# Cross-attention and expert layer: one token tile and one value tile per attention step, and one row-maximum instruction for both heads of a step

## The reference, cut to what matters

```python
x = x + tanh(g_xattn[0]) * xattn(layernorm(x), ctx_1024, Wq, Wk, Wv, Wo, bo)   # (8, 512, 512), 8 heads of 64
x = x + tanh(g_ffn[0])   * moe(layernorm(x), gate_w, Wu, Wv, Wo)               # 8 experts, rank 128, 2 chosen per token

# xattn
q, k, v = x @ Wq, context @ Wk, context @ Wv        # split into 8 heads of 64
attn = softmax(q k^T / 8)                           # 512 x 512 per batch row and head
out  = (attn v) @ Wo + bo
```

## Time and profile before

| what | value |
|---|---|
| median of 3 runs | 1095.46 us (1092.81 to 1096.62) |
| the profiled execution, its own time | 1095.08 us |
| its span in the trace | 1093.3 us |
| TensorE busy | 901.7 us, 82% of the span |
| VectorE busy | 682.8 us |
| ScalarE busy | 571.8 us |
| GpSimd busy | 540.2 us |
| attention steps 0 to 31 in the trace | from 51.3 us to about 767 us |

### The profile page before, as it was taken

The page is one execution under the profiler, slowest core; times in us unless marked ns, Lnnn a source line. Parts: engine busy times, 40 slices in busy tenths (PEclk is TensorE's granted clock), DMA queues, the critical chain, the costliest instruction groups (busy, mean ns, idle before and its releaser), DMA issues.

```text
span 1093.3 us, 22768 instructions
## 1 busy us (share of the span) xinstructions
PE 901.7 (82%) x8210; PEld 547.0 (50%) x8210; DVE 682.8 (62%) x1595; ACT 571.8 (52%) x1022; POOL 540.2 (49%) x645
## 2 busy tenths in 40 slices
PE   4888988998998899899899989986640999799890
PEld 2344444555455455455555545544320787677660
DVE  5677776677687767867767776685334454444440
ACT  3367656666457555655754655656120564555450
POOL 6222253353565466447545544547463246556564
PEclk9999999999999999999999999999765899899995
DMA  8455734645453264354336226643343589899986
GB/s 264 143 165 176 236 117 99 191 108 127 128 145 74 66 192 108 67 174 113 74 91 200 69 59 189 185 117 125 103 145 116 139 186 197 167 187 187 196 143 84
DMA packets 125997, 154.52 MB, mean 141 GB/s; under 512 B 48448, under 2 KB 81216, under 8 KB 125120
## 3 DMA queue, kind: packets, MB, share of 16 engines
q1 hardware_dynamic: 109024, 115.67, 37.0%
q0 software_dynamic: 16864, 37.40, 17.8%
HBM read 67.06 MB, written 56.56 MB: 113 GB/s over the span
## 4 chain that ended last, share of the span: by engine, by line
PE 53%; DVE 13%; DMA 10%; issue 9%; ACT 7%; POOL 4%; SPq 2%; POOLq 1%; ACTq 0%; DVEq 0%
PE G L1244 27%; DMA out_dram<-V,Ph 8%; PE ST L1301 4%; PE ST L1300 4%; PE MX L1286 3%; PE MX L1468 3%; PE G L1253 3%; POOL out_dram L673 3%; DVE mx L884 2%; PE PV L1317 2%; PE PV L1313 2%; PE PV L1315 2%; DVE tiles L874 2%; PE G L1460 1%; ACT Ph L708 1%
## 5 line engine op out<-in xcount | busy, mean ns | idle before, releaser
L630 POOL TENSOR_TENSOR Pl<-P,Ph 128x512 f16<-128x512 f32 x128 | 153.4, 1202 | 215.5 <-ACT Ph L708 215.0
L705 ACT ACTIVATE P<-ST 128x512 f32<-128x512 f32 x256 | 153.3, 599 | 201.4 <-PE ST L1301 166.8
L884 DVE TENSOR_REDUCE mx<-MX 128x1 f32<-128x512 f32 x256 | 168.2, 684 | 26.7 <-PE MX L1286 26.7
L708 ACT ACTIVATE Ph<-ST 128x512 f16<-128x512 f32 x256 | 154.3, 603 | 0.4
L673 POOL DMA_INDIRECT out_dram<-V,Ph x78 | 122.1, 1566 | 47.4 <-ACT V L841 30.1
L1468 PE MATMUL MX<-heads,tiles 128*128 128x256 f16 x936 | 121.5, 283 | 18.5 <-DVE heads L1198 18.2
L1313 PE MATMUL PV<-V,Ph 128*128 128x65 f16 x1024 | 114.4, 195 | 12.2 <-issue 12.2
L1317 PE MATMUL PV<-V,Pl 128*128 128x65 f16 x1024 | 114.4, 194 | 2.7 <-issue 2.6
L1315 PE MATMUL PV<-V,Ph 128*128 128x64 f16 x1024 | 114.6, 197 | 0.9 <-issue 0.9
L1313 PEld LDWEIGHTS PV<-V,Ph 128*128 128x128 f16 x1024 | 97.5, 98 | 34.3 <-issue 16.5
L1468 PEld LDWEIGHTS MX<-heads,tiles 128*128 x936 | 92.3, 101 | 41.4 <-issue 23.0
(11 more groups left out here) (206 smaller groups left out, 1895.4 us busy)
## 6 DMA issues: line engine op xcount, KB each, us to landing
heads<-expert_rows SPq DMA_DIRECT2D x39, 516.0 KB
tiles<-in_x_dram SPq DMA_DIRECT2D x32, 256.0 KB, 5.1
tiles<-in_ctx_dram SPq DMA_DIRECT2D x32, 256.0 KB, 5.2
second_norm<-in_x_dram SPq DMA_DIRECT2D x32, 256.0 KB, 3.2
out_dram<-second_norm SPq DMA_DIRECT2D x32, 256.0 KB, 2.3
heads<-q_hi SPq DMA_DIRECT2D x124, 64.0 KB
heads<-k_hi SPq DMA_DIRECT2D x124, 64.0 KB
expert_rows<-zero_rows SPq DMA_DIRECT2D x8, 516.0 KB, 5.3
```

What stands on the lines that cost most here:

```text
L630: nc.gpsimd.tensor_tensor(Pl[:, hh, c, :], P32[:, c, :], Ph[:, hh, c, :], ALU.subtract).then_inc(pl_pool, 1)
L705: nc.scalar.activation(P32[:, c, :], ST[:, c % 2, :], ACT.Exp, scale=0.125 / SC2).then_inc(p_ready, 1)
L708: nc.scalar.activation(Ph[:, hh, c, :], ST[:, c % 2, :], ACT.Exp, scale=0.125 / SC2).then_inc(ph_ready, 1)
L884: nc.vector.tensor_reduce(out=mx[:, k // TT, k % TT:k % TT + 1], in_=MX[:, (k + odd) % 2, :], axis=AXX, op=ALU.max).then_inc(mx_taken, 1)
```

## The change

Four things are done together.

1. **Token and value tiles.** From step 2 on every step prepares one token tile (tile g + 6) and, from step 4 on, one value tile (tile g + 4); steps 0 and 1 keep two token tiles, steps 2 and 3 two value tiles. The sums over the kernel are the same. The token tile's x transposes stand after S6, its context transposes after half of the weighted sums, the value tile at the end of the step. Loads, layernorm statistics and factors are made tile by tile, not batch row by batch row.
2. **Row maxima.** The two heads' products of a token block are issued one behind the other into the two banks, each over its own 64 partitions, and one VectorE instruction reduces both banks (128 x 2 x 512). Four reductions stand where eight stood. The low part of k no longer enters the maximum.
3. **Order around the general banks.** The output projection, the ranks and the tiles change places in `bank_uses`; the transpose of the maxima stands before the logits; in steps j = 1 the ranks follow the output projection. On ScalarE the high part of oT moves behind one more pair of exponentials, and the high parts of the tile behind another.
4. **Ranking on VectorE.** `best_two` moves from before the low part of oT to after the token tile's low parts; `places` moves from the end of step j = 1 into step j = 2, after two of the four reductions.

```diff
+def token_tiles(g, steps):
+
+    first, second = ([4 + 2 * g], [5 + 2 * g]) if g < 2 else ([g + 6], [])
+    return [n for n in first if n < steps], second
+
+
+def value_tiles(g, steps):
+
+    if g < 4:
+        return [2 * g, 2 * g + 1] if g >= 2 else []
+    return [g + 4] if g + 4 < steps else []
...
@@ bank_uses
+        first, second = token_tiles(g, steps)
+        names += [(z, n) for n in first for z in "xc"]
+        if b:
+            names.append(("out", g - 4))
+        names += [(z, n) for n in second for z in "xc"]
         if j == 1 and b >= 2:
             names.append(("ranks", b - 2))
-        if b:
-            names.append(("out", g - 4))
-        names += second
+        names += [("v", n) for n in value_tiles(g, steps)]
...
@@ vector engine
-            def row_max(n, k, odd):
-                dve.wait_ge(mx_filled, n + 1)
-                nc.vector.tensor_reduce(out=mx[:, k // TT, k % TT:k % TT + 1], in_=MX[:, (k + odd) % 2, :], axis=AXX,
+            def row_max(n, t):
+
+                dve.wait_ge(mx_filled, n)
+                nc.vector.tensor_reduce(out=mx[:, :, t:t + 1].rearrange("p h o -> p (h o)"), in_=MX[:], axis=AXX,
                                         op=ALU.max).then_inc(mx_taken, 1)
...
@@ tensor engine
             def row_max_scores(g, k):
...
-                h, t = k // TT, k % TT
+                t, h = divmod(k, 2)
+                rows_ = slice(h * HD, (h + 1) * HD)
                 if k == 0:
                     pe.wait_ge(qk_dma[s], turn * QK_DMAS * 16)
                 if k == 1:
                     since(pe, mrow_ready, g)
                 else:
-                    since(pe, mx_taken, g * (2 * TT) + k - (1 if k > 1 else 0))
-                nc.tensor.matmul(MX[:, (k + g) % 2, :], Q1[:, s, h, t * P:(t + 1) * P], K1[:, s, h, :],
+                    since(pe, mx_taken, g * TT + t)
+                nc.tensor.matmul(MX[:, h, :], Q1[rows_, s, h, t * P:(t + 1) * P], K1[rows_, s, h, :],
                                  start=True, stop=True).then_inc(mx_filled, 1)
...
@@ tensor engine, step
-                    maxima(2 * k)
+                    maxima(2 * k, 2 * k + 1)
...
-                maxima(2 * k + 1)
...
                 scores(b, j, 4)
                 last_head(2, 3)
+                scores(b, j, 5)
+                if g < STEPS - 1:
+                    max_transpose(g + 1)
...
-                if g < STEPS - 1:
-                    max_transpose(g + 1)
-                scores(b, j, 5)
-                if more:
-                    side(ahead)
                 scores(b, j, 6)
+                for n in first:
+                    x_tile(n)
                 weighted(hd, 0)
                 weighted(hd, 1)
-                if j == 1 and b >= 2:
-                    ranks(b - 2)
+                for n in first:
+                    c_tile(n)
+                scores(b, j, 7)
...
                 if b:
                     out_project(g - 4)
-                scores(b, j, 7)
                 weighted(hd, 2)
                 weighted(hd, 3)
-                if more:
-                    side(ahead + 1)
+                for n in second_:
+                    x_tile(n)
+                    c_tile(n)
+                if j == 1 and b >= 2:
+                    ranks(b - 2)
+                for n in value_tiles(g, STEPS):
+                    v_tile(n)
```

More of the change, by code:

```diff
@@ L463, in step @@
                     sp.wait_ge(qk_dma[1], QK_DMAS * 16)
+                if g in (1, 2):
+                    for n in (2 * g + 6, 2 * g + 7):
+                        sp.wait_ge(filled, use["c", n - TT] + 1)
+                        load_tile(*divmod(n, TT))
                 if b == 0:
@@ L492, in step @@
                     turn(g - 5)
-                if j == 2 and b < B - 2:
-                    for t in range(TT):
-                        load_tile(b + 2, t)
+                if g >= 3 and g + 9 < TILES:
+                    sp.wait_ge(filled, use["c", g + 5] + 1)
+                    load_tile(*divmod(g + 9, TT))
                 if b:
@@ L784, in step @@
                 hd = b * HB + 2 * j
-                ahead = 4 * (b + 1) + 2 * (j % 2)
-                def side(n):
-                    turned_hi(n) if j < 2 else v_hi(n)
+                first, second_ = token_tiles(g, STEPS)
                 exps(hd, 0, 0, 1)
@@ L795, in step @@
                     piece_hi(3 * j)
-                if more and j < 2:
-                    for n in (ahead, ahead + 1):
-                        normalise(n)
+                for n in first + second_:
+                    normalise(n)
                 if proj:
@@ L1122, in step, with maxima @@
                 mxn = (g + 1) * (2 * TT + 1)
-                odd = (g + 1) % 2
                 nmax = g < STEPS - 1
-                ahead = 4 * (b + 1) + 2 * (j % 2)
-                def maxima(*ks):
-                    for k in ks:
+                first, second_ = token_tiles(g, STEPS)
+                def maxima(*ts):
+                    for t in ts:
                         if nmax:
-                            row_max(mxn + k, k, odd)
-                def side(n):
-                    turned_lo(n) if j < 2 else v_lo(n)
-                maxima(0, 1, 2, 3)
+                            row_max(mxn + 2 * t + 2, t)
+                maxima(0, 1)
                 probs_lo(hd, 0, 0)
+                if j == 2 and b >= 2:
+                    places(b - 2)
+                if g == 10:
+                    outsiders()
                 if proj:
                     lo_part(("q", g), native["q"][1][:], native["q"][0][:], QS)
-                maxima(4, 5)
+                maxima(2)
                 probs_lo(hd, 0, 1)
-                maxima(6, 7)
+                maxima(3)
                 if nmax:
-                    negate((g + 2) * (2 * TT))
+                    negate((g + 2) * TT)
                 if proj:
@@ L1160, in step @@
                     piece_lo(3 * j + 1)
-                if more:
-                    side(ahead)
-                if j == 3 and b < B - 2:
-                    for t in range(TT):
-                        statistics(TT * (b + 2) + t)
+                if b:
+                    lo_part(("oT", g - 4), oT[1][:], oT[0][:], 1.0)
                 probs_lo(hd + 1, 1, 1)
+                for n in first:
+                    turned_lo(n)
+                if g and g + 7 < TILES:
+                    tile_statistics(g + 7)
                 if j == 1 and b >= 2:
-                    take_ranks(b - 2)
+                    best_two(b - 2)
                 if b:
@@ L1173, in step @@
                     piece_lo(3 * j + 2)
-                if more:
-                    side(ahead + 1)
+                for n in second_:
+                    turned_lo(n)
                 if j == 1 and b >= 2:
-                    places(b - 2)
-                if g == 9:
-                    outsiders()
+                    take_ranks(b - 2)
+                for n in value_tiles(g, STEPS):
+                    v_lo(n)
             for b in range(B):
@@ L1266, in v_tile @@
             def v_tile(n):
+                if n >= TT:
+                    pe.wait_ge(evacuated, use["c", n] + 1)
                 product(bank(("v", n)), v_parts(n)).then_inc(filled, 1)
```

87 lines of the change are left out of this document (50 added, 37 removed).

## The result

The changed kernel takes **1107.88 us** (median of 6 runs, 1103.92 to 1114.14) against 1095.6 us (1090.18 to 1096.62) for the kernel before: **1.0139 times as long, 95% interval 1.0105 to 1.0173**. Forecast were 1076.5 us and faster. The profiled execution has an own time of 1113.48 us and a span of 1111.8 us, 18.5 us over the span before.

What follows compares the result with a forecast made beforehand. The prediction took TensorE's own stream plus short waits to bound the attention stage. It summed 1095.08 - 23.7 (row-maximum pairs) + 5 (new order) = 1076.4, stated as 1076.5 us, range 1056 to 1108.

Steps and rivals of the forecast that it cites:

- Term 1: Row-maximum products: 128 pairs on separate partition halves run side by side, each saving 0.216 - 0.031 us; -23.7 us.
- So I take 0 for a change of shape: Row-maximum pairs: switching the array into halves and back, twice per pair, costs nothing; far end +42 us.
- term 2: New order in steps 8 to 27: waits of 11.9 us per batch row against 10.8 now; +5 us over five.
- The second rival: Row-maximum pairs: each of 256 shape changes runs TensorE empty, exposing 0.164 us; +42, 1118 us; decides from 0.09; chance 0.17.
- the half price: Row-maximum pairs: each shape change costs half the empty-array price, 0.08 us; +21, 1097 us; chance 0.12.
- the walk: Step-by-step timing of the new order in steps 8 to 27: TensorE waits 11.9 us per batch row, good to 3.
- Steps 0 to 7 and 28 to 31: First and last attention steps: the same work changes neighbours; 0 us, with 5 us either way.
- the fourth rival: Row-maximum pairs still run in turn, so their gain is 0 and 1100 us remain; chance 0.12.

Runs made afterwards that it cites:

- e2: Changed kernel with both row-maximum products of a pair over partitions 0 to 63 of head 0, so they run in turn; 1116.16 us, 1.0323 of the kernel before.
- e1: Changed kernel with its row-maximum products over all 128 partitions again, joint reduction kept; 1104.95 us, 1.0181 of the kernel before.
- e5: Changed kernel with `places` and the unit list's arithmetic back at the end of step j = 1; 1088.78 us, 0.9963 of the kernel before.
- e8: Changed kernel with high parts of oT and the tile's x before the moved exponentials, x's low part before the probabilities' low part; 1079.64 us, 0.9895 of before.
- e9: e8 with `places` and the unit list's arithmetic moved behind the tile's statistics in step j = 2; 1062.26 us, 0.9695 of the kernel before.
- e10: e9 with the rank products of steps j = 1 moved behind the value tile; 1051.8 us, 0.9607 of the kernel before.
- e0: The changed kernel run again unaltered, on the chip of the runs beside it; 1107.75 us, 1.0123 of the kernel before.
- e4: Changed kernel with a batch row's first scatter back in the middle of step j = 2; 1094.85 us, 1.0132 of the kernel before.
- e11: e10 with row-maximum products over all 128 partitions; 1053.37 us, 0.9630 of the kernel before.

## Why the prediction was wrong

**Term 1 failed, and with it the sign.** The step that failed is "So I take 0 for a change of shape". The first half of the term was right: the two products start together and the second adds nothing measurable, a gain of 0.21 us per pair. Part 3 of the Trainium skill's page "TensorE: Matmul & The Clock Gate" puts the starts of matmuls on different row groups about 4 ns apart; the trace agrees, with 3 ns at 307.29. The second half was priced by the wrong neighbour. The earlier trace rows show a transpose with fewer columns and no gap; the change here is of rows, and it costs 0.09 to 0.12 us each way (0.31 and 0.33 in place of 0.216; e2 against e1 confirms the sum of the two). 128 x (0.21 - 0.21) = 0 instead of -23.7, and with the +5 of term 2 that alone turns the forecast to 1100, slower than before. The Trainium skill's page "TensorEngine Tiling (Array Packing)", section Tiling Modes, says that such a switch drains TensorE. The trace agrees for rows, at two thirds of the 0.164 that I took for an empty array; for the columns of the earlier trace rows it shows no gap. The second rival named the mechanism, and its turning point, 0.09 per change, lay right at the measured price. It got 0.17, and the half price, 0.08, 0.12; both were underweighted because one row on another dimension was read as evidence against them.

**Term 2 was nearly right in size.** Batch row 4 (steps 16 to 19) loses 1.4 to 1.5 four times, 0.47 four times, 0.75 in j = 1 and 2.1 in j = 2, 10.7 us where the walk had 11.9. It also loses 1.8 in j = 3, which the walk lacks: 12.5 in all. The term was +5 us, the window shows +8.5. Missing in it:
- the wait in steps j = 3. I followed the scatter along GpSimd's own queue only and did not ask who stands still beside it. The standstill was there in the trace before, at 389.7; the change moved work that TensorE needs soon into its reach. That follows from the times; no run shows it by taking the scatter away on a chip that has the standstill.
- the unit list's arithmetic in step 10, behind `places`: 4.3 us of wait at the third pair instead of 2.4.
- the clock: a wait of 2 us and more can be followed by a stretch at the lower level, 1.9 us in step 14.

**"Steps 0 to 7 and 28 to 31: 0, with 5 us either way"** were 3.7 and 3.5 us. Each is inside its bound; both have the same sign. In step 1, for example, TensorE now waits 2.2 us for ScalarE's exponentials.

**The sum.** Against the profiled execution: 23.7 (term 1), 3.5 (term 2), 7.2 (outer steps), 2.9 (start and rest) come to 37.3, and between 1076.4 and 1113.48 lie 37.1 (the rest is rounding). By medians the miss is 31.4 us, and term 1 is three quarters of it. The range, 1056 to 1108, ends 0.1 above the median. That it holds the median is luck and no credit to the mechanism: its upper end was set by the half price (1097) and the fourth rival (1100), and neither came true as it stands. The second rival's sum with the measured 0.105 us per change gives 1103.

**What I had wrong about the pieces.** The 2.4 us of `places` were in the sum, but I set them against waits of the old order and called the balance +5. e5 shows that this one move costs about 1.6%, as much as the whole loss or a little more; the rest of the new order pays for itself. Cutting the two chains (e8), putting `places` and the ranks where VectorE or TensorE has other work (e9, e10), turns the new order from 1.2% slower to 3.9% faster.

## What to carry to other kernels

Price a change of the array's row shape before splitting matmuls over halves: here it ate the whole overlap of a pair of 512 columns. More such work per change could leave a gain, but no run here tries it. When long plain chains of small VectorE operations must go somewhere, put them where the tensor engine has a long stretch that does not need VectorE, and never between the reductions that free its banks; count a wait of two microseconds as up to four. When two operand chains feed consecutive products, shorten both or neither.

## What the runs showed of the hardware that was not expected

- Two 64-row products into two banks run side by side: 0.39 us for the pair. Entering and leaving the 64-row shape costs about 0.1 us each (0.31 and 0.33 us in place of 0.216; e2 against e1: 0.84 against 0.64). A matmul with 8 columns in place of 128 costs nothing.
- In some runs ScalarE, and in part VectorE, stand still beside a group of four indirect scatters of GpSimd, ScalarE until about 1 us past their end, and the views name no releaser that they know ("remote"): 31.2 us of ScalarE's idle time in steps 8 to 27 of the kernel before ended so, 29.6 in e0 and e5, and none in e1 to e4 on another chip. In e8 to e11, whose scatters stand in the same place, ScalarE loses nothing by it, and VectorE about 3 us.
- It is TensorE's signals that are late there. In the trace's semaphore records of steps 8 to 27, 23 signals of TensorE come 0.5 us and more after the drawn end of their matmul in the kernel before, up to 2.4 us; in the changed kernel 19, up to 3.4 us; in e8 to e11 7 to 10 each; in e1 to e4 none. Those of ScalarE, VectorE and GpSimd come within 0.02 us of their instruction's end where the trace records both. A matmul's end is modelled, but matmuls behind it start on time. What holds the signals is open. That it is the scatter is a guess from the times alone.
- The same wait is sometimes followed by a stretch at 1.2 GHz and sometimes not: step 14 lasts 26.28 us in the changed kernel and 24.65 in e0, the same kernel, with 2.24 us of wait in both; step 9 of e9 lasts 23.01, steps 13, 17, 21 and 25 25.14 to 25.17.
